# Computing only the routed token-expert pairs in two mixtures of experts

## The reference

```python
# layer 0
probs = softmax(xf @ router_w.T); topv, topi = top_k(probs, 2)
topv = topv / (topv.sum(-1) + 1e-09)
h = gelu(einsum('td,edh->teh', xf, w1))        # hidden 512, all 8 experts
out = einsum('te,ted->td', cw, einsum('teh,ehd->ted', h, w2))
# layer 3
gates = sigmoid(xf @ Wg); vals, idx = top_k(gates, 2); vals = vals / vals.sum(-1)
shared = silu(xf @ Ws1) * (xf @ Ws3) @ Ws2     # hidden 256, every row
h = silu(einsum('td,edf->tef', xf, We1)) * einsum('td,edf->tef', xf, We3)
out = (shared + einsum('tef,efd,te->td', h, We2, w)) / 3
```

## Time and profile before

| | |
|---|---|
| median of 3 runs | 2128.96 us (2127.35 to 2130.54) |
| span of the profiled execution | 2126.5 us |
| TensorE busy | 1874.9 us, 88% of the span |
| VectorE busy | 1221.3 us, 57% |
| ScalarE busy | 863.8 us, 41% |
| GpSimd busy | 584.6 us, 27% |
| DMA | 18.81 MB, mean 9 GB/s |

### The profile page before, as it was taken

How to read it: one execution, slowest core, us unless ns; L and a number is a source line. 1 busy time by engine, 2 the same in 40 slices (tenths; PEclk the granted TensorE clock), 3 DMA queues, 4 the chain that set the end, 5 groups by cost and what they waited for, 6 DMA issues and landing times. The chain is left out here.

```text
span 2126.5 us, 38848 instructions
## 1 busy us (share of the span) xinstructions
PE 1874.9 (88%) x13151; PEld 1551.1 (73%) x13151; DVE 1221.3 (57%) x2828; ACT 863.8 (41%) x1957; POOL 584.6 (27%) x823
## 2 busy tenths in 40 slices
PE   4888899999999678578777888699999997999999
PEld 3777689999998656466665444578778876888888
DVE  3777632223222879666676788455545554666665
ACT  2555544444443433344433333344454453333332
POOL 1444430000000335333333333245445444000000
PEclk9999999999999579788888899899999998999999
DMA  5000020000000000000000000000000002000000
GB/s 149 1 0 0 6 75 1 1 1 0 0 1 1 0 1 1 1 0 0 0 0 1 0 0 0 1 0 0 0 0 0 0 0 67 6 6 11 5 6 11
DMA packets 28641, 18.81 MB, mean 9 GB/s; under 512 B 3220, under 2 KB 26956, under 8 KB 28429
## 3 DMA queue, kind: packets, MB, share of 16 engines
q1 hardware_dynamic: 24498, 16.11, 2.6%
q10 hardware_dynamic: 4059, 1.60, 0.3%
HBM read 15.61 MB, written 2.10 MB: 8 GB/s over the span
## 5 line engine op out<-in xcount | busy, mean ns | idle before, releaser
L838 PEld LDWEIGHTS psum<-w_down_ffn,hidden_ffn 128*128 128x128 f32 x3200 | 377.8, 192 | 11.4
L838 PE MATMUL psum<-w_down_ffn,hidden_ffn 128*128 128x128 f32 x3200 | 378.6, 275 | 0.0
L780 DVE SCALAR_TENSOR_TENSOR x_residual<-psum,expert_weight_ffn,x_residual 128x128 f32<-128x128 f32 (+1 forms) x544 | 153.2, 344 | 319.2 <-PE psum L838 318.9
L356 POOL TENSOR_TENSOR exp_scores<-exp_scores,softmax_recip 128x308 f32<-128x308 f32 x256 | 181.7, 741 | 316.1 <-DVE softmax_recip L457 316.1
L810 PE MATMUL psum<-xt_high_ffn,w_up_low_ffn 128*128 128x512 f32 x544 | 228.1, 419 | 4.8 <-POOL w_up_high_ffn L652 4.6
L685 ACT ACTIVATE hidden_ffn<-psum 128x512 f32<-128x512 f32 x256 | 150.0, 600 | 185.1 <-PE psum L810 172.3
L810 PE MATMUL psum<-xt_low_ffn,w_up_high_ffn 128*128 128x512 f32 x544 | 216.2, 398 | 0.0
L810 PE MATMUL psum<-xt_high_ffn,w_up_high_ffn 128*128 128x512 f32 x544 | 216.1, 397 | 0.0
L688 ACT ACTIVATE silu_ffn<-psum 128x512 f32<-128x512 f32 x144 | 85.3, 597 | 211.3 <-PE psum L810 209.6
L660 POOL TENSOR_TENSOR xt_low_ffn<-xt_ffn,xt_high_ffn 128x512 fp32r<-128x512 f32 x16 | 20.6, 1288 | 544.2 <-ACT xt_high_ffn L697 544.1
L474 PE MATMUL psum<-identity,exp_scores 128*77 128x128 f32 x1024 | 151.4, 295 | 4.6 <-POOL exp_scores L356 3.9
(11 more groups left out here) (282 smaller groups left out, 3475.6 us busy)
## 6 DMA issues: line engine op xcount, KB each, us to landing
x_residual<-in_x_dram SPq DMA_DIRECT2D x4, 512.0 KB, 11.8
w_up_raw_ffn<-in_L_ffn_w_dram SPq DMA_DIRECT2D x8, 256.0 KB, 2.8
w_down_ffn<-in_L_ffn_w_dram SPq DMA_DIRECT2D x8, 256.0 KB, 3.2
w_up_raw_ffn<-in_L_ffn_We_dram SPq DMA_DIRECT2D x16, 128.0 KB, 2.1
out_dram<-x_residual SPq DMA_DIRECT2D x8, 256.0 KB, 2.3
context_rows<-in_ctx_dram ACTq DMA_DIRECT2D x1, 1232.0 KB
L_wkv<-in_L_xattn_Wkv_dram SPq DMA_DIRECT2D x1, 1024.0 KB
w_down_ffn<-in_L_ffn_We_dram SPq DMA_DIRECT2D x8, 128.0 KB, 2.2
```

The costliest lines, as they stand in the source:

```text
L356: nc.gpsimd.tensor_tensor(e[:, par, heads, :], e[:, par, heads, :], rec.to_broadcast([S, HG, KC]), ALU.mult).then_inc(s["probs_ready"], 1)
L780: ins = nc.vector.scalar_tensor_tensor(m.x[:, group * GB + t, :], m.psum[:, 4 + (p * n_exp + e) % 2, t * D:(t + 1) * D], weight[:, p, e, t ...
L838: mm = nc.tensor.matmul(m.psum[:, 4 + slot, t * D:(t + 1) * D], hid[:, slot, c, t * S:(t + 1) * S], down[:, e, c, :], start=(c == 0), stop ...
```

## The change

`experts` is replaced by `sparse_experts` for both mixtures. The 32 batches are two halves of 16. For each half a list of slots is made in DRAM (`sorted_x`), sorted by expert, and each expert's part is rounded up to tiles of 256 slots. Since 4096 pairs of a half need at most 16 + 7 tiles, there are always 23 per half, 46 per mixture; slots that no pair takes keep what was there before.

The steps of the new stage:

- All 32 batches are normalised, transposed and given logits first, in 8 groups. Then each half is routed in one go, with operations four times as wide. Each pair's slot comes from two small matmuls that count rows (`earlier`, `all_ones`), a scan over batches, and a scan over experts. The expert of each tile is written to an SBUF row.
- POOL scatters the normalised rows: 32 indirect DMAs per half (16 batches, 2 picks), each of 128 rows of 512 bytes.
- For each tile SP reads the expert's number into a register, loads that expert's weights from DRAM (256 + 256 KB in layer 0, three times 128 KB in layer 3) and the tile's 256 rows (128 KB), in one of three slots; TensorE transposes the rows, computes the hidden features in plain float32 (four products of 256 columns), and the output; DVE copies the transposed rows and the output from PSUM to SBUF; SP stores the output to DRAM (`sorted_y`, 128 KB).
- POOL gathers each batch's two result rows back (32 indirect DMAs per half), and DVE adds both, weighted, to the residual. The first half's batches are combined one after each of tiles 27 to 42, the second half's after the last tile.
- The shared expert of layer 3 is computed in plain float32 for all 8 groups, between routing and the first tile.
- `prepare` also builds the constants and clears both `sorted_x` lists, with four DMAs of 1.5 MB that the stage waits for, behind the later loads on SP's queue.

The core of the diff (the routing arithmetic and the semaphore names are left out):

```diff
+HALVES = 2
+HBATCH = B // HALVES
+TILE = 256
+TILES = HBATCH * S * 2 // TILE + E0 - 1
+SLOTS = TILES * TILE
...
+            sync.wait_ge(zero_ready, 1)
+            for half in range(HALVES):
+                for q in range(SLOTS // (128 * SLOT_ROWS)):
+                    rows = m.sorted_x[half][q * 128 * SLOT_ROWS:(q + 1) * 128 * SLOT_ROWS, :].rearrange("(p r) d -> p r d", p=128)
+                    sync.dma_start(rows, m.zeros[:, :, :]).then_inc(cleared, 16)
...
+            sync.wait_ge(cleared, 16 * (HALVES * SLOTS // (128 * SLOT_ROWS)))
...
+                def load(n):
+                    k, half, j = n % 3, n // TILES, n % TILES
+                    if j == 0:
+                        sync.wait_ge(s["tiles_known"], half + 1)
+                    e = sync.value_load(expert[0:1, half, j:j + 1], min_val=0, max_val=E0 - 1)
+                    if n >= 3:
+                        sync.wait_ge(s["y_in_psum"], n - 2)
+                    sync.dma_start(wu[:, k, 0, :], w_up(e)).then_inc(tile_loaded[k], 16)
+                    if sides == 2:
+                        sync.dma_start(wu[:, k, 1, :], w_gate(e)).then_inc(tile_loaded[k], 16)
+                    sync.dma_start(wd[:, k, :, :], w_down(e).rearrange("(c f) d -> f c d", f=128)).then_inc(tile_loaded[k], 16)
+                    if j == 0:
+                        sync.wait_ge(scattered[half], 16 * 2 * HBATCH)
+                    sync.dma_start(xs[:, k, :, :], m.sorted_x[half][j * TILE:(j + 1) * TILE, :].rearrange("(u p) d -> p u d", p=128))\
+                        .then_inc(tile_loaded[k], 16)
+
+                def keep(n):
+                    sync.wait_ge(s["y_ready"], n + 1)
+                    sync.dma_start(m.sorted_y[n // TILES][n % TILES * TILE:(n % TILES + 1) * TILE, :].rearrange("(u p) d -> p u d", p=128), y[:, n % 2, :, :])\
+                        .then_inc(y_stored[n % 2], 16)
+
+                for n in range(NTILES + 2):
+                    if n < NTILES:
+                        load(n)
+                    if n >= 2:
+                        keep(n - 2)
...
+                for half in range(HALVES):
+                    pool.wait_ge(s["ranked"], half + 1)
+                    for b in range(HBATCH):
+                        for k in range(2):
+                            nc.gpsimd.indirect_dma_start(m.sorted_x[half][:, :], bass.IndirectOffsetOnAxis(slot[:, half, k, b:b + 1], 0),
+                                                         xn[:, half * HBATCH + b, :], None).then_inc(scattered[half], 16)
+                for half in range(HALVES):
+                    done = (half + 1) * TILES
+                    pool.wait_ge(y_stored[0], 16 * ((done + 1) // 2))
+                    pool.wait_ge(y_stored[1], 16 * (done // 2))
+                    for b in range(HBATCH):
+                        n = half * HBATCH + b
+                        if n >= 4:
+                            pool.wait_ge(s["combined"], n - 3)
+                        for k in range(2):
+                            nc.gpsimd.indirect_dma_start(yg[:, n % 4, k, :], None, m.sorted_y[half][:, :],
+                                                         bass.IndirectOffsetOnAxis(slot[:, half, k, b:b + 1], 0)).then_inc(gathered[n % 4], 16)
...
+                def transposes(n):
+                    pe.wait_ge(tile_loaded[n % 3], 16 * LOADS * (n // 3 + 1))
...
+                transposes(0)
+                up(0)
+                transposes(1)
+                for n in range(NTILES):
+                    if n + 1 < NTILES:
+                        up(n + 1)
+                    if n + 2 < NTILES:
+                        transposes(n + 2)
+                    down(n)
...
+                transposed(0)
+                if layer == 3:
+                    gated(0)
+                transposed(1)
+                for n in range(NTILES):
+                    if n + 1 < NTILES and layer == 3:
+                        gated(n + 1)
+                    if n + 2 < NTILES:
+                        transposed(n + 2)
+                    dve.wait_ge(s["y_in_psum"], n + 1)
+                    if n >= 2:
+                        dve.wait_ge(y_stored[n % 2], 16 * (n // 2))
+                    nc.vector.tensor_copy(y[:, n % 2, :, :], m.psum[:, 4 + n % 2, 0:TILE].rearrange("p (u d) -> p u d", d=D)).then_inc(s["y_ready"], 1)
+                    if HALVES > 1 and COMBINE_FROM <= n < COMBINE_FROM + HBATCH:
+                        combine(n - COMBINE_FROM)
+                for n in range(B - HBATCH, B):
+                    combine(n)
```

More of the change, by code:

```diff
@@ L37 @@
 VPAD = D // HG + DK
+HALVES = 2
[3 more added lines that the diff above has]
+SLOTS = TILES * TILE
+SLOT_ROWS = 23
 def wait(eng, sem, value):
@@ L601, in experts @@
[L601 to L624 removed]
+        xn = sb("xn", [S, B, D])
@@ new lines, in sparse_experts @@
+        count = sb("expert_tiles", [S, E0])
+        first = sb("expert_first_tile", [S, E0])
+        last = sb("expert_tiles_upto", [S, E0])
+        rank = sb("slot_by_expert", [S, E0, HBATCH])
+        product = sb("slot_products", [S, HBATCH, E0])
+        slot_f = sb("slot_float", [S, 2, HBATCH])
+        slot = sb("slot", [S, HALVES, 2, HBATCH], mybir.dt.uint32)
+        weight = sb("expert_weight", [S, HALVES, 2, HBATCH])
+        work_row = sb("tile_experts_passed", [1, TILES])
+        passed = sb("tile_passed", [1, TILES, E0])
@@ L705, in _ @@
-                pipeline(act, step, NGB)
+                for g in range(NGB):
+                    act.wait_ge(s["xt_in_psum"], g + 1)
+                    if g >= 2 and not shared:
+                        act.wait_ge(s["logits_in_psum"], g - 1)
+                    at = g if shared else g % 2
+                    nc.scalar.copy(xts[:, at * GT:(at + 1) * GT], m.psum[:, 6 + g % 2, :]).then_inc(s["xts_ready"], 1)
+                for half in range(HALVES):
+                    act.wait_ge(s["exp_wanted"], half + 1)
+                    nc.scalar.activation(probs[:, half, :, :], probs[:, half, :, :], ACT.Exp,
+                                         scale=1.0 if layer == 0 else -1.0).then_inc(s["exp_ready"], 1)
@@ new lines, in _ @@
+                preload(nc, m, ACT.Gelu if layer == 0 else ACT.Silu)
+                if shared:
+                    for g in range(NGB):
+                        for c in range(chunks):
+                            act.wait_ge(s["shared_hidden"], g * chunks + c + 1)
+                            if g * chunks + c >= 2:
+                                act.wait_ge(s["shared_hid_ready"], g * chunks + c - 1)
+                            nc.scalar.activation(ssilu[:, c, :], m.psum[:, c, :], ACT.Silu).then_inc(s["shared_silu"], 1)
@@ L859, in _ @@
-                pipeline(pe, step, NGB)
+                for g in range(NGB):
+                    pe.wait_ge(s["xn_ready"], g + 1)
+                    if g >= 2:
+                        pe.wait_ge(s["xts_ready"], g - 1)
+                    for t in range(GB):
+                        mm = nc.tensor.transpose(m.psum[:, 6 + g % 2, t * S:(t + 1) * S], xn[:, g * GB + t, :], m.ident[:, :])
+                    mm.then_inc(s["xt_in_psum"], 1)
+                    pe.wait_ge(s["xts_ready"], g + 1)
+                    half, at = g // (NGB // HALVES), g % (NGB // HALVES)
+                    row = g if shared else g % 2
+                    for t in range(GB):
+                        mm = nc.tensor.matmul(m.psum[:, 4 + half, (at * GB + t) * E0:(at * GB + t + 1) * E0],
+                                              xts[:, row * GT + t * S:row * GT + (t + 1) * S], router_t[:, :], start=True, stop=True)
+                    mm.then_inc(s["logits_in_psum"], 1)
@@ new lines, in down @@
+                def down(n):
+                    pe.wait_ge(s["hidden_ready"], (n + 1) * (2 if layer == 0 else 1))
+                    if n >= 2:
+                        pe.wait_ge(s["y_ready"], n - 1)
+                    for u in range(TILE // 128):
+                        for c in range(chunks):
+                            mm = nc.tensor.matmul(m.psum[:, 4 + n % 2, u * D:(u + 1) * D], hid[:, n % 2, c, u * 128:(u + 1) * 128],
+                                                  wd[:, n % 3, c, :], start=(c == 0), stop=(c == chunks - 1))
+                    mm.then_inc(s["y_in_psum"], 1)
```

459 lines of the change are left out of this document (234 added, 225 removed).

## The result

| | before | after |
|---|---|---|
| median of four runs | 2129.09 us (2127.35 to 2130.54) | 2514.91 us (2503.46 to 2518.74) |
| span of the profiled execution | 2126.5 us | 2516.8 us |
| granted clock, mean | 0.945 | 0.814 |

The ratio is 1.180, 95% interval 1.177 to 1.183: slower by 386 us, where the prediction had 2420 us in a range of 2200 to 2640. The direction, the bound and the mechanism came out as forecast; the sum of the terms was 290 us and the spans differ by 390.

What follows compares the result with a forecast made beforehand. The prediction took each tile's load chain, not TensorE, as the bound; first mixture +136, second +128 and program start +26 made +290 on 2126.5, 2417, and 2420 us with 2.5 added for the median; range 2200 to 2640.

Steps and rivals of the forecast that it cites:

- The bound: In the tile loops, three slots give no depth, so each tile's load latency stands open: 5.6 and 5.3 us a tile.
- Rival 1: Tile loops: TensorE stays the bound, loads land under the up projection, periods 3.9 and 3.0 us, 1964 us; chance 0.08.
- point of decision: Test for TensorE staying the bound: both periods together must be under 10.5 us; the forecast's lowest was 13.0.
- The clock: TensorE in the tile loops: three quarters at 1.2 GHz, periods 9.4 and 7.4 us, loops 432 and 340 us.
- rival 3: Tile loops: all of it at 1.2 GHz, periods 9.9 and 7.7 us, 2457 us; chance 0.13.
- The register read: SP reading each tile's expert number before its loads: 0.7 us plus 0.1 for the address, between 0.07 and 2.3.
- The indirect DMAs: POOL's scatters and gathers: 1.27 us each, so 32 take 40.6 us.
- Rival 4: POOL's indirect DMAs at 2.5 us each, pacing on POOL at both ends: +144 us, 2564 us; chance 0.15.
- Ahead of the loop: Transposes and logits of eight groups, routing, scatters and first load before the first mixture's loop: 83 us.
- Behind the loops: After each loop, last copy and store, 32 gathers, landing and last combine: 47 us first mixture, 50 second.
- Program start: Four clears of 1.5 MB behind the later loads on SP, which the stage waits for: +26 us.
- the scatter hides under: Second mixture: the scatter hides under TensorE's shared expert, with 97 us in all ahead of the loop.

Runs made afterwards that it cites:

- experiment 3: Changed kernel with each tile's down projection put ahead of the transposes that wait for a load, VectorE's copies likewise, still three buffers: 2161.9 us.
- experiment 7: Experiment 3's kernel with four buffers in place of three for a tile's weights and rows: 2150.1 us.
- all: Experiment 7's kernel plus experiment 4's paced scatters, and GpSimd instead of SyncE waiting for the clears, ahead of its first scatter: 2059.3 us.
- experiment 4: Changed kernel with the second half's scatters sent two at a time, one pair per finished tile; the first half's stay a burst: 2427.2 us.
- Experiment 2: Changed kernel with seven useless float32 matmuls a tile filling TensorE's wait for the load: 2338.2 us.
- experiment 6: Changed kernel with each tile's expert number written into the program, so SyncE reads no register and works out no address: 2445.1 us.
- 5: Changed kernel rerun unaltered, 2525.6 us; and with waits at experiment 4's places on a count reached long before, so no pauses, 2516.3 us.
- experiment 9: Changed kernel with each scatter of the second half waiting until the one before it has landed: 2457.0 us.
- experiment 10: As `all` but transposes ahead of the down projection, plus a wait after every fourth scatter in the second mixture's first run: 2023.2 us.
- experiment 1: Changed kernel with only the first mixture sorted, the second being that of the kernel before: 2292.9 us.

## Why the prediction was right, and where it was short

- **The bound.** That TensorE does not stay the bound, because a load is only asked for when the down projection three tiles before is done and copied out: shown by experiment 3 (some 250 us from the order alone), by experiment 7 (regular periods of 4.63 and 3.73 us with a fourth buffer) and by the links of the chain, 5.74 us for 5.6. Rival 1 had the right arithmetic. Its point of decision was 10.5 us for both periods; the changed kernel has 17.2, experiment 3's 11.1 and is slower than before still (by 1.6%), `all` 8.4 and is faster. Experiment 7's has 8.4 as well and is no faster than before (ratio 1.009): the stalls, which the point of decision left out, take it back. A tile's own work is 4.0 and 3.1 us (the periods less the 0.63 of wait for the transposed rows), against 3.9 and 3.0 in the sum.
- **The clock.** Three quarters of the tiles at 1.2 GHz, periods of 9.4 and 7.4: measured 9.88 and 7.35 as medians, granted clock 0.71 and 0.78. The first tiles were quick, so that without the stall the first loop is 428 us (experiment 4) from first to last transposes, where 45 x 9.4 = 423 was the forecast: this term was right to 5 us. The rule of the Trainium skill (TensorE: Matmul & The Clock Gate, "HAM oscillation — how this bites in real kernels"), rival 3, gave 9.9 and 7.7. It fits the first loop's median but not its length (45 x 9.9 = 446 for 428), and overstates the second, whose first half had a median period of 6.82. That the second loop's 7.35 is so near 7.4 is partly luck: its first half had a tail of 1.33 us, which is the 2.4 GHz level, and a chain of 5.47 in the median, its second half, with the gathers beside it, a tail of 2.30 and a chain of 5.97, where the forecast had one chain of 5.3 all through. Experiment 2 shows the effect by itself: with the wait filled, the clock is 0.99 and the tail shrinks as worked out.
- **The register read.** Taken at 0.7 + 0.1 between ends of 0.07 and 2.3; 0.75 in the trace, 0.71 by experiment 6. The total is right and its split is not: the read is 0.27 us, less than an issue of 0.37, where the prediction argued that it must be dearer than one; the address and what stands around it are the rest.
- **The indirect DMAs.** Taken at 1.27 each from a GpSimd pass that has nothing to do with them; they stand 1.26 apart (0.96 and a gap of 0.30), scatters and gathers alike. The value is right; that the row was a good guide is luck. Rival 4 (2.5 us) is out.
- **Ahead of the loop.** Groups of 3.50 us, all at the slow clock (window 0.50), so 28 for the 24 taken; 86 for 83. Behind the loops 51 for 47: the next stage begins 5.4 us after the last combine. Program start 21 for 26.
- **The step that failed** is the sentence that the second half's scatter lies beside 20 tiles "and cost[s] nothing; [its] cover would go only above 4 us each", and with it that in the second mixture "the scatter hides under" the shared expert. GpSimd had the time, as predicted. But a long unbroken run of scatters held all other engines up: 35 us in the first loop, which was 40 over, and 67 on the way to the second, which was 63 over. Without the stalls the kernel is at 2427 us (experiment 4), 7 from the 2420 predicted. I had counted a hidden stretch as an engine's time alone and asked only what it needs, not what it takes from others.
- **The range.** Its ends do not follow from the terms given for them: the two favourable ends with a fast clock come to 2420 - 58 - 84 - 115 = 2163, not 2200, and the two dear ones to 2420 + 147 + 144 = 2711, not 2650. The measured time lies well inside either. It also lies 5 us above the 2340 to 2510 that the forecast gave as its own range, because of the stalls, which no rival named.

**What stays open.** That pauses in the run take the stall away is shown by experiment 4 with 5 as its control, and by 9 inside one program; 10 agrees. Every stall lay beside an unbroken run of scatters or just behind it. It is not sufficient: in experiments 1, 2 and 3 the runs were unbroken and nobody was held up, in both mixtures, where these were sorted. The first half's runs of experiment 4 are unbroken too and held nobody up. The stall came in both executions of the changed kernel that were profiled, so it is a property of the program and not of the moment. A trait goes with it in the DMA records: the fetches of instructions. Of the window 376 to 412 us the changed kernel's table of queues has two rows, and that of experiment 3, whose first run of scatters is at the same place, four (packets, MB, share of the DMA engines' time):

```profile
q0 software_dynamic: 849, 1.71, 14.5%
q1 hardware_dynamic: 944, 0.66, 6.5%
```

```profile
q1 hardware_dynamic: 6789, 4.32, 40.8%
q0 software_dynamic: 899, 1.84, 14.9%
q8 instruction: 1, 0.02, 0.2%
q14 instruction: 1, 0.01, 0.1%
```

In the five kernels with a stall in the first loop the first fetch after 314 us comes at 393 to 448, in the five others with the same start at 383 to 387; in the second mixture the five have none for 94 to 96 us, where the kernels of experiments 2 and 3 have one on queue q8 every 26 to 42. Engines that are short of instructions would look just so: idle for nothing that is shown, and going on in steps of 0.70 us. That is argued from records that coincide, not shown; why a fetch gets through in one program and not in another was not tried. Two records speak against the fetch as the start of it. Experiment 4 has a gap of 61 us on q8 (2068 to 2129) in the second loop and no tile above 8.8. And in the changed kernel SyncE's issues of one tile already stand 1.4 us apart at 373 us, 10 us before the first fetch of the undisturbed kernels:

```profile
372.60 0.00 SPq L656 DMA_DIRECT2D tile_w_down_ffn<-in_L_ffn_w_dram  x1
373.99 0.70 SPq L659 DMA_DIRECT2D sorted_rows_ffn<-sorted_x  x1
```

In experiment 1 the same two issues of the same tile are 0.45 us apart, at 371.35 and 371.80. So a late fetch may as well be a consequence of the hold-up as its cause.

## What to carry to other kernels

Sorting for fewer operations pays only if the loop that replaces the dense one is deep enough: count for each buffer the time from its release to its next filling, and compare it with the work that stands between. Here a fourth buffer, pauses in a run of indirect DMAs, and a later wait for the clears (16 us of it) turned an 18% loss into a 5% gain with the same arithmetic. And work on an idle engine is not free because that engine has time; look in the trace after for other engines' idle time that nothing explains.

## What the runs showed of the hardware

- 32 indirect scatters of 128 rows of 512 B, issued without a pause, can hold every other engine up until 5 to 11 us after the end of the last (ScalarE's next instruction in the eight kernels with a stall); in other programs the same run holds nobody up. With a pause after each (1.5 us or more, experiment 9) or after every fourth (1.5 us, experiment 10) there was no stall.
- The gathers, the same instruction in the other direction and also 1.25 us apart, held nobody up. Beside the loops at most 8 of them stand in an unbroken row, since they wait for combines. Behind each loop all 32 are unbroken (gaps of 0.30 us), and VectorE's combines kept pace, one every 2.3 to 2.6 us; TensorE and ScalarE had no work there, so for them it is not shown.
- Seven useless matmuls a tile (0.45 us each, 280 us in all) made the kernel faster, some 75 us of it by the clock as estimated above, since they stood in a wait.
- A scatter lands 2.2 us after its issue and a gather 2.6 (medians of experiment 3; the slowest 4.5 and 4.7). The Trainium skill (DMA: Bandwidth & Descriptors, "Anatomy of one DMA — SWDGE (gpsimd) path") fits 2.0 us plus bytes over 436 GB/s; for 64 KB that is 2.15 as an estimate. The trace agrees for the scatters, and the gathers take 0.45 us more.
